# A fused cross-attention and FP4 feed-forward kernel: last rows in two half blocks, first block by feature chunks, small work on GpSimd, softmax ahead of quantisation

## The chip, the core and the metric

The kernel runs on one core of one Trainium2 chip. The metric is the device time of one execution in microseconds (us); runs are compared by their medians. TensorE is called PE here, VectorE DVE, ScalarE ACT, GpSimd POOL and SyncE SP.

## What is computed

The input x has 2 x 2048 rows of 512, and each of the two batches has 77 text tokens. Every row is layer-normalised, projected, and compared with each token of its batch by an additive attention score: a tanh of a 512-vector, dotted with w. The softmax over the tokens gives two numbers, a gate and a shift, for the row. Then a gated feed-forward layer (512 to 1408 to 512) runs on values quantised to FP4 in blocks of 16.

```python
txt_proj = einsum('btd,de->bte', ctx, Ws);  feat_proj = einsum('bfd,de->bfe', layernorm(x), W)
h = tanh(txt_proj[:, None] + feat_proj[:, :, None] + b)      # rows x 77 tokens x 512
rho = einsum('bftd,d->bft', h, w) - 1e30 * (1 - mask)
txt_h = softmax(rho) @ ctx
x = x + tanh(txt_h . Wcw + bcw) * layernorm(x) + tanh(txt_h . Wcb + bcb)
# fp4(v): per block of 16: scale = max|v| / 6; v / scale to the nearest of 0, .5, 1, 1.5, 2, 3, 4, 6; times scale
n = fp4(layernorm(x));  g = n @ fp4(w_gate).T;  y = n @ fp4(w_up).T
x = x + fp4(silu(g) * y) @ fp4(w_down).T
```

## The kernel before

**Scores.** The rows are cut into blocks (`BLOCKS`, line 26: four of 1024). The features of a row lie transposed in `featT`, in 4 chunks of 128 partitions; the token's part is a bias per partition. A quad is four tanh instructions of ACT (`tanh_quad`, line 425; 128 x the block's rows each) and the matmuls that dot them with w (`score_quad`, line 537). A quad of 1024 rows has 8 matmul instructions, one of 512 rows would have 4; each is two passes in the trace. A block needs 77 quads (`QPB`) whatever its rows. The tanh results pass through a ring of four places of 512 rows (`hring`): two quads of 1024 rows, or four of 512.

**The feed-forward tiles.** There are 32 tiles of 128 rows. A tile has four gate/up slots (p = 0 to 3, `gate_up`, line 602, 24 matmuls each) and three down slots (p = 4 to 6, `down`, line 615, 33 matmuls in all) for the tile before. DVE prepares the rows (`rows_tile`), multiplies SiLU(gate) by up (`hidden`), quantises (`quantise`, line 679; `quantise_hidden`) and adds the result. SP moves the quantised rows through transposing DMAs (`turn_x`, `turn_h`).

**The order of work** is written out by hand. Each engine runs its own list and waits on semaphores. `slots` (lines 77 to 92) spreads the quads of block k over the slots of the tiles before it: those of block k end at slot 2 of tile `BASE[k] - 2`, and those of the next begin at slot 5 of the same tile. ACT issues up to two quads beyond what PE scores in a slot, before that slot's SiLU (line 472). In tile `BASE[k] - 2` the scores of the block are drained from PSUM (`softmax_drain`), transposed on PE (`softmax_transposes`), shifted by their maximum (`softmax_shift`), and in the next tile summed (`softmax_sums`) and turned into per-row factors (`softmax_factors`), which `rows_tile` of the next block needs.

**The first block** has no tiles beside it. PE turns its rows, projects the text and the four chunks of both halves (`project_head`, order in `FEAT`, line 250), and then scores. Beside the first block's quads lie the preparation of the weights and of the other 24 tiles' features, taken in 12 pairs of tiles (`rows_pair`, `turn_pair`, `copy_pair`, `project_pair`, `features_pair`), one pair every 4.5 quads (line 584), and on DVE the quantisation of 22 weight pieces of 512 columns and 4 of 1408 (lines 831 to 842). Only when all of them are turned (`wd_turned`, line 842) does DVE drain the first block's scores. GpSimd only builds two small constant tables at the start.

`quantise` forms the block scale, its reciprocal and, in lines 699 to 701, the split of the scale into two float16 parts:

```python
step(stt(d, s, SPLIT, s, ALU.mult, ALU.subtract))
step(stt(hi_b, s, SPLIT, d, ALU.mult, ALU.subtract))
step(tt(lo_b, s, hi_b, ALU.subtract))
```

Lines 716 and 717 need the parts, seven instructions further on.

## Time and profile before

| | us |
|---|---|
| median of 3 runs (lowest, highest) | 1726.71 (1726.48, 1731.03) |
| the profiled execution | 1726.88 |
| its span, first to last instruction | 1725.1 |
| ACT busy in the span | 1356.6 (79%) |
| PE busy | 1482.5 (86%) |
| DVE busy | 1103.6 (64%) |
| POOL busy | 2.7 |

Rows of the trace give a start time in us from the span's start, a busy time in us, the engine, the line of the kernel, what is written and read, and how many instructions are merged (x). A bracket behind a row is the idle time in front of it and the instruction that ended it. Stages are told as stretches of the span: to 62 the head, to 415 the first block, to 1445 the three other blocks beside tiles 0 to 22, and after it the tiles that have no tanh beside them.

### The profile page before, as it was taken

What the parts mean: (1) busy time and instruction counts of PE and PEld (TensorE: products, weight loads), DVE (VectorE), ACT (ScalarE), POOL (GpSimd) and SP (SyncE); (2) the same over time, 40 slices, a digit from 0 to 9 for tenths busy, and PEclk for the clock granted to TensorE, in tenths of its full rate; (3) what the DMA queues carried; (4) which work ended last, traced back from release to release, by engine and by line L of the source; (5) the groups of instructions that cost most, each with busy time, mean ns of one, the idle gap of its engine ahead of it and who ended that gap; (6) DMA issues with size and microseconds to landing.
All of it is one profiled execution on the core that took longest, in us unless ns stands there. A gap on an engine that the chain in (4) does not pass through costs nothing.

```text
span 1725.1 us, 23814 instructions
## 1 busy us (share of the span) xinstructions
PE 1482.5 (86%) x9752; PEld 650.2 (38%) x9752; DVE 1103.6 (64%) x1983; ACT 1356.6 (79%) x1398; POOL 2.7 (0%) x18
## 2 busy tenths in 40 slices
PE   5788888766889989888999999899999998688895
PEld 4234444311333333343333333433333334355552
DVE  4679999864474445356655555657555556799994
ACT  1798888899999999969999999799999995100000
POOL 0000000000000000000000000000000000000000
PEclk9999899888999999999999999999999999799997
DMA  4122232331011111210221111102211111132312
GB/s 130 37 61 71 73 70 68 83 63 30 13 24 36 36 24 36 36 36 13 59 34 39 36 36 36 31 9 45 36 36 36 36 36 36 36 71 61 69 42 52
DMA packets 180753, 77.87 MB, mean 45 GB/s; under 512 B 163851, under 2 KB 163851, under 8 KB 180645
## 3 DMA queue, kind: packets, MB, share of 16 engines
q1 hardware_dynamic: 177392, 74.99, 19.4%
q10 hardware_dynamic: 3253, 1.37, 0.3%
q8 instruction: 76, 1.25, 0.3%
q14 instruction: 32, 0.26, 0.0%
HBM read 27.85 MB, written 8.39 MB: 21 GB/s over the span
## 4 chain that ended last, share of the span: by engine, by line
ACT 59%; DVE 27%; PE 11%; issue 1%; ACTq 1%; DMA 1%; DVEq 0%; SPq 0%
ACT hring L438 56%; DVE work L703 4%; PE rho L548 3%; DVE work L714 2%; DVE work L715 2%; DVE sm L694 2%; ACT sg L458 2%; DVE work L908 1%; DVE work L712 1%; DVE work L713 1%; DVE sm L697 1%; PE dn L623 1%; DVE work L717 1%; DVE work L716 1%; DVE bn L754 1%
## 5 line engine op out<-in xcount | busy, mean ns | idle before, releaser
L438 ACT ACTIVATE hring<-featT,bias 128x1024 f32<-128x1024 f32 x1232 | 1293.0, 1141 | 78.2 <-PE rho L548 73.5
L548 PE MATMUL rho<-hring,wslide 128*32 128x512 f32 x4928 | 618.9, 626 | 135.1 <-ACT hring L438 135.1
L548 PEld LDWEIGHTS rho<-hring,wslide 128*32 128x32 f32 x4928 | 133.5, 112 | 503.3 <-ACT hring L438 274.4
L623 PE MATMUL dn<-wd_room,turned 128*128 128x512 f16 x1056 | 243.9, 383 | 12.8 <-DMA turned<-work 12.8
L908 DVE TENSOR_TENSOR work<-sg,gu1u 128x352 f32<-128x352 f32 x64 | 33.4, 521 | 298.5 <-ACT sg L458 298.0
L623 PEld LDWEIGHTS dn<-wd_room,turned 128*128 128x128 f16 x1056 | 99.2, 99 | 174.7 <-issue 54.8
L611 PE MATMUL gu0g<-wg,turned 128*128 128x352 f16 x768 | 129.6, 320 | 35.7 <-DVE work L908 19.7
L458 ACT ACTIVATE sg<-gu0g 128x352 f32<-128x352 f32 x64 | 29.0, 453 | 153.3 <-PE gu0u L611 153.2
L611 PE MATMUL gu1g<-wg,turned 128*128 128x352 f16 x768 | 128.3, 318 | 0.0
L611 PE MATMUL gu0u<-wu,turned 128*128 128x352 f16 x768 | 126.2, 315 | 0.0
L611 PE MATMUL gu1u<-wu,turned 128*128 128x352 f16 x768 | 125.0, 313 | 0.0
L908 DVE TENSOR_TENSOR work<-sg,gu0u 128x352 f32<-128x352 f32 x64 | 33.4, 521 | 139.7 <-ACT sg L458 138.6
L611 PEld LDWEIGHTS gu0g<-wg,turned 128*128 128x128 f16 x768 | 72.0, 99 | 114.8 <-issue 37.5
L611 PEld LDWEIGHTS gu1g<-wg,turned 128*128 128x128 f16 x768 | 72.5, 99 | 77.4 <-issue 40.9
L703 DVE TENSOR_TENSOR work<-work,sm 128x1408 f32<-128x1408 f32 x34 | 93.9, 2762 | 1.2
L611 PEld LDWEIGHTS gu0u<-wu,turned 128*128 128x128 f16 x768 | 75.8, 99 | 40.5
L611 PEld LDWEIGHTS gu1u<-wu,turned 128*128 128x128 f16 x768 | 75.1, 98 | 39.4
L458 ACT ACTIVATE sg<-gu1g 128x352 f32<-128x352 f32 x64 | 29.1, 454 | 68.0 <-PE gu1u L611 68.0
L714 DVE TENSOR_TENSOR work<-work 128x1408 f32<-128x1408 f32 (+1 forms) x56 | 70.5, 1259 | 1.9
L715 DVE TENSOR_TENSOR work<-work 128x1408 f16<-128x1408 f32 (+1 forms) x56 | 70.5, 1258 | 1.9
L694 DVE TENSOR_REDUCE sm<-work 128x88 f32<-128x1408 f32 x34 | 55.1, 1620 | 1.2
L697 DVE RECIPROCAL sm<-sm 128x88 f32<-128x88 f32 (+1 forms) x90 | 44.4, 493 | 3.1
(147 smaller groups left out, 1019.6 us busy)
## 6 DMA issues: line engine op xcount, KB each, us to landing
xt<-in_x SPq DMA_DIRECT2D x32, 256.0 KB, 2.9
out<-xt SPq DMA_DIRECT2D x32, 256.0 KB, 2.3
work<-in_x SPq DMA_DIRECT2D x10, 512.0 KB, 4.6
xt<-in_x SPq DMA_DIRECT2D x6, 512.0 KB, 3.8
xt<-in_L_ffn_w_gate SPq DMA_DIRECT2D x11, 256.0 KB, 2.6
xt<-in_L_ffn_w_up SPq DMA_DIRECT2D x11, 256.0 KB, 3.5
work<-in_L_ffn_w_down SPq DMA_DIRECT2D x2, 704.0 KB, 4.3
xt<-in_L_ffn_w_down SPq DMA_DIRECT2D x2, 704.0 KB, 4.9
```

What stands on the lines that cost most here:

```text
L438: act.activation(hring[:, s // 2, g, (s % 2) * 512:(s % 2) * 512 + rows], featT[:, e, ROW0[k]:ROW0[k] + rows], ACT.Tanh, bias=bias[:, e, b ...
L458: act.activation(sg[:, n % 2, :], gu[n % 2][0][:, 0:GU_N], ACT.Silu, scale=1.0 / W_PRE).then_inc(sg_ready, 1)
L548: last = pe.matmul(rho[SLOTW * g:SLOTW * g + SLOTW, hf * 512:hf * 512 + 512], wslide[:, e, SLOTW - 1 - r:2 * SLOTW - 1 - r], hring[:, s // ...
L611: last = pe.matmul(ps[:, 0:GU_N], xqT[:, a, k, :], w[:, bb, k, n * GU_N:n * GU_N + GU_N], start=(k == 0 and i == 0), stop=(k == KC - 1 and ...
L623: last = pe.matmul(dn[:, :], hqT[:, a, c, :], wd[:, bb, c, :], start=(c == 0 and i == 0), stop=(c == NC - 1 and i == 2))
L694: step(dve.tensor_reduce(am, v, axis=AX_X, op=ALU.max, apply_absolute_value=True))
L697: step(dve.reciprocal(r, s))
L703: ins = tt(a.rearrange("p (i q b) -> p i b q", **natural), src.rearrange("p (i b q) -> p i b q", **natural), r.rearrange("p (i b) -> p i b ...
L712: step(ts(m.bitcast(I32), a.bitcast(I32), 0x7F800000, None, ALU.bitwise_and))
L714: step(tt(a, a, m, ALU.add))
L715: step(tt(q, a, m, ALU.subtract))
L908: signal(tt(h, sg[:, n % 2, :], gu[n % 2][1][:, 0:GU_N], ALU.mult), gu_drained[n % 2], 2 * t + n // 2 + 1)
```

## The change

`BLOCKS` becomes (1024, 1024, 1024, 512, 512): the last 1024 rows are two blocks, of tiles 24 to 27 and 28 to 31. A quad of the two small blocks has tanh instructions of 128 x 512. The first block's quads run chunk by chunk (`quad_at`), and of the projections only chunk 0 and half of chunk 1 stand ahead of the first score; the others, the text projections of chunks 1 to 3 and the one for the gates stand between quads. A pair of tiles comes every 5 quads from quad 8 on. GpSimd splits the scales of all 90 quantisations and normalises the rows of the pairs, with DVE computing only their statistics. Small loads are issued by SP instead of ACT. In the tile where a block's quads end, drain, transposes and shift stand ahead of `quantise_hidden`, and the next block's quads begin at slot 3.

```diff
-BLOCKS = (1024, 1024, 1024, 1024)
+BLOCKS = (1024, 1024, 1024, 512, 512)
 PRE_QUADS = 7
...
-        if q < 2 * KC:
-            return q % 2, q // 2
+        if q < KC * KC:
+            return q % KC, q // KC
         return q // KC, q % KC
...
-        t0, p0 = (0, 0) if k == 1 else (BASE[k - 1] - 2, 5)
+        t0, p0 = (0, 0) if k == 1 else (BASE[k - 1] - 2, 3)
...
+        feat_bank = [[gu[1][0][:, :], gu[1][1][:, :]], [tr[:, :], dn[:, :]]]
+        text_bank = [gu[0][e % 2][:, 0:BATCH * TOK] for e in range(KC)]
+        uv_bank = gu[0][0][:, 0:2 * BATCH * TOK]
...
+            for n, src in enumerate((w_in, b_in, Wcw_in, Wcb_in)):
+                flat = src.rearrange("a b -> (a b)")
+                sp.dma_start(cols[:, n, :], flat.rearrange("(k p) -> p k", p=P),
+                             allow_slow_non_contiguous=True).then_inc(loaded_c, 16)
+            for n, src in enumerate((bcw_in, bcb_in)):
+                sp.dma_start(bc[:, n:n + 1], src.rearrange("(a n) -> a n", a=1).broadcast_to([P, 1])).then_inc(loaded_c, 16)
...
+            def split(n):
+
+                nb = n // QB
+                s, t, d = sm[:, 1, 0:nb], split_t[:, 0:nb], split_d[:, 0:nb]
+                splits[0] += 1
+                pool.wait_ge(scale_ready, splits[0])
+                small(pool.tensor_scalar(t, s, SPLIT, 1.0, ALU.mult, ALU.mult))
+                small(pool.tensor_tensor(d, t, s, ALU.subtract))
+                small(pool.tensor_tensor(s_hi[:, 0:nb], t, d, ALU.subtract))
+                pool.tensor_tensor(s_lo[:, 0:nb], s, s_hi[:, 0:nb], ALU.subtract).then_inc(split_ready, 1)
+                pool.wait_ge(split_ready, splits[0])
+
+            def normalise_pair(p):
+
+                pool.wait_ge(pair_stats, p + 1)
+                t0 = HEAD_T + 2 * p
+                for j in range(2):
+                    pool.tensor_scalar(xpair[p % 2][:, j, :], xpair[p % 2][:, j, :], nmean[:, j:j + 1],
+                                       rstd[:, t0 + j:t0 + j + 1], ALU.add, ALU.mult).then_inc(pair_normal, 1)
+                pool.wait_ge(pair_normal, 2 * p + 2)
+
+            normalise_pair(0)
+            split(D)
+            split(D)
+            for w in range(1, NC):
+                split(D)
+                normalise_pair(w)
+                split(D)
+            normalise_pair(NC)
+            for r in range(KC):
+                split(INNER)
+            split(D)
+            for t in range(NT):
+                if t + 1 < NT:
+                    split(D)
+                split(INNER)
+
...
-            for e in range(KC):
-                act.wait_ge(text_filled, e // 2 + 1)
-                act.activation(bias[:, e, :], gu[0][e // 2][:, (e % 2) * BATCH * TOK:(e % 2 + 1) * BATCH * TOK],
-                               ACT.Identity, bias=cols[:, 1, e:e + 1]).then_inc(bias_ready, 1)
+            act.wait_ge(text_filled, 1)
+            act.activation(bias[:, 0, :], text_bank[0], ACT.Identity, bias=cols[:, 1, 0:1]).then_inc(bias0_ready, 1)
             copy_head(1)
-            act.wait_ge(bias_ready, KC)
+            act.wait_ge(bias0_ready, 1)
...
-                if k == 0 and q < 2 * KC and q % 2 == 0:
-                    act.wait_ge(feat_ready, feat_at(q // 2))
+                if k == 0 and q < KC * KC and q % KC == 0:
+                    act.wait_ge(feat_ready, 2 * (q // KC) + 2)
+                    if q > 0:
+                        act.wait_ge(bias_ready, q // KC)
...
+                    if t - 1 in SOFTMAX_AT and n == 0:
+                        softmax_exp(SOFTMAX_AT[t - 1])
                     silu_gate(t, n)
-                    if t - 1 in SOFTMAX_AT and n == 1:
-                        softmax_exp(SOFTMAX_AT[t - 1])
...
+            project_text(0)
             pe.wait_ge(loaded_w, 16)
-            pe.wait_ge(bias_ready, KC)
-            project_head(0)
-            project_head(1)
+            project_head(0, 0)
             turn_head(1)
-            for i in range(2, len(FEAT)):
-                project_head(i)
...
+            project_head(0, 1)
+            project_text(1)
+            project_head(1, 0)
...
-                pe.wait_ge(xn_ready, HEAD_T + 2 * p + 2)
+                pe.wait_ge(pair_normal, 2 * p + 2)
                 if p == 0:
-                    pe.wait_ge(uv_ready, 1)
...
+                if n == 0:
+                    project_head(1, 1)
+                if n == 2:
+                    project_text(2)
+                    project_head(2, 0)
+                if n == 3:
+                    project_head(2, 1)
+                if n == 5:
+                    project_text(3)
+                    project_head(3, 0)
+                if n == 6:
+                    project_head(3, 1)
+                if n == 7:
+                    project_uv()
                 for w in range(PAIRS + 1):
-                    at = 5 + (9 * w) // 2
+                    at = 8 + 5 * w
...
-                    if t in SOFTMAX_AT and p == 5:
+                    if t in SOFTMAX_AT and p == 3:
                         softmax_transposes(SOFTMAX_AT[t], 0)
-                    if t - 1 in SOFTMAX_AT and p == 0 and halves(SOFTMAX_AT[t - 1]) == 2:
-                        softmax_transposes(SOFTMAX_AT[t - 1], 1)
                     for n in slots.get((t, p), ()):
                         score_quad(n)
+                    if t in SOFTMAX_AT and p == 3 and halves(SOFTMAX_AT[t]) == 2:
+                        softmax_transposes(SOFTMAX_AT[t], 1)
...
+                scales[0] += 1
+                signal(ts(s, am, pre / FP4_MAX, least * pre, ALU.mult, ALU.max), scale_ready, scales[0])
                 step(dve.reciprocal(r, s))
                 step(ts(r, r, pre * TIE_DOWN, None, ALU.mult))
-                step(stt(d, s, SPLIT, s, ALU.mult, ALU.subtract))
-                step(stt(hi_b, s, SPLIT, d, ALU.mult, ALU.subtract))
-                step(tt(lo_b, s, hi_b, ALU.subtract))
 
...
+                dve.wait_ge(split_ready, scales[0])
...
-            rows_pair(0)
-            for w in range(NC + KC):
-                if w < NC:
-                    gate_up_weights(w)
-                else:
-                    down_weights(w - NC)
-                if w < PAIRS:
-                    copy_pair(w)
-                if 0 < w <= PAIRS:
-                    features_pair(w - 1)
-                if w + 1 < PAIRS:
-                    rows_pair(w + 1)
...
+            gate_up_weights(0, 0)
+            text_bias(2)
+            features_head(2)
+            gate_up_weights(0, 1)
+            text_bias(3)
+            features_head(3)
+            text_gates()
+            for w in range(NC - 1):
+                copy_pair(w)
+                gate_up_weights(w + 1, 0)
+                stats_pair(w + 1)
+                if w > 0:
+                    features_pair(w - 1)
+                gate_up_weights(w + 1, 1)
+            copy_pair(NC - 1)
+            stats_pair(NC)
+            features_pair(NC - 2)
+            down_weights(0)
+            copy_pair(NC)
+            features_pair(NC - 1)
+            down_weights(1)
+            down_weights(2)
+            features_pair(NC)
+            down_weights(3)
...
                 hidden(t, 0)
-                if ending is not None and halves(ending) == 2:
-                    softmax_shift(ending, 1)
                 hidden(t, 1)
                 if ending is not None:
                     softmax_sums(ending)
                 elif t + 1 < NT:
                     rows_tile(t + 1)
                 hidden(t, 2)
+                if begun is not None:
+                    softmax_drain(begun)
+                    softmax_shift(begun, 0)
                 hidden(t, 3)
+                if begun is not None and halves(begun) == 2:
+                    softmax_shift(begun, 1)
                 if ending is not None:
                     softmax_factors(ending)
                     rows_tile(t + 1)
-                if begun is not None:
-                    softmax_drain(begun)
                 quantise_hidden(t)
                 if t > 0:
                     result(t - 1)
                 if begun is not None:
-                    softmax_shift(begun, 0)
                     restart()
             result(NT - 1)
 
```

**On PE, at the start of the program** (gu, tr and dn are PSUM banks; stage and wd_room hold the turned rows of the two halves, turned holds W). Before:

```order
L517 MATMUL gu0g<-wd_room 128x154 x8
L517 MATMUL gu0u<-wd_room 128x154 x8
L507 MATMUL gu0g<-stage,turned 128x512 x4
L507 MATMUL gu1g<-stage,turned 128x512 x4
L507 MATMUL gu0u<-wd_room,turned 128x512 x4
L507 MATMUL gu1u<-wd_room,turned 128x512 x4
L507 MATMUL gu0g<-stage,turned 128x512 x4
L507 MATMUL gu0u<-wd_room,turned 128x512 x4
L507 MATMUL gu1g<-stage,turned 128x512 x4
L507 MATMUL gu1u<-wd_room,turned 128x512 x4
L532 MATMUL tr<-wd_room,xt 128x154 x8
L548 MATMUL rho<-hring,wslide 32x512 x48
```

In the change:

```order
L573 MATMUL gu0g<-wd_room 128x154 x4
L563 MATMUL gu1g<-stage,turned 128x512 x4
L563 MATMUL gu1u<-wd_room,turned 128x512 x4
L573 MATMUL gu0u<-wd_room 128x154 x4
L563 MATMUL tr<-stage,turned 128x512 x4
L609 MATMUL rho<-hring,wslide 32x512 x8
L563 MATMUL dn<-wd_room,turned 128x512 x4
L609 MATMUL rho<-hring,wslide 32x512 x16
L573 MATMUL gu0g<-wd_room 128x154 x4
L563 MATMUL gu1g<-stage,turned 128x512 x4
```

Ahead of the first score stand three half chunks of 128x512 in place of eight, and two text projections of 128x154 x4 in place of four; five half chunks and two text projections went between the first quads.

**On DVE, around the drain of a block's scores in tile 6.** Before:

```order
L908 TENSOR_TENSOR work<-sg,gu1u 128x352
L847 TENSOR_SCALAR stage<-rho,negm 128x1024
L694 TENSOR_REDUCE sm<-work 128x88
...
L716 TENSOR_TENSOR work<-work,s_hi 128x1408
L717 TENSOR_TENSOR work<-work,s_lo 128x1408
L920 SCALAR_TENSOR_TENSOR xt<-dn,xt 128x512
L854 TENSOR_REDUCE mx<-tr 128x4
L855 TENSOR_TENSOR stage<-tr,mx 128x512
L908 TENSOR_TENSOR work<-sg,gu0u 128x352
L854 TENSOR_REDUCE mx<-tr 128x4
L855 TENSOR_TENSOR stage<-tr,mx 128x512
```

In the change:

```order
L1013 TENSOR_TENSOR work<-sg,gu0u 128x352
L952 TENSOR_SCALAR stage<-rho,negm 128x1024
L959 TENSOR_REDUCE mx<-tr 128x4
L960 TENSOR_TENSOR stage<-tr,mx 128x512
L1013 TENSOR_TENSOR work<-sg,gu1u 128x352
L959 TENSOR_REDUCE mx<-tr 128x4
L960 TENSOR_TENSOR stage<-tr,mx 128x512
L769 TENSOR_REDUCE sm<-work 128x88
...
L791 TENSOR_TENSOR work<-work,s_lo 128x1408
L1025 SCALAR_TENSOR_TENSOR xt<-dn,xt 128x512
```

Both shifts moved ahead of the 14 (now 11) instructions of the quantisation and of the result, and the drain moved ahead of the second half's last `hidden` product.

**On ACT, in tiles 14 to 22 and 22 to 26 of the change** (sg is the SiLU of a gate/up slot). In the first stretch:

```order
L516 ACTIVATE sg<-gu0g 128x352
L496 ACTIVATE hring<-featT,bias 128x512 x4
L516 ACTIVATE sg<-gu1g 128x352
L496 ACTIVATE hring<-featT,bias 128x512 x8
L516 ACTIVATE sg<-gu0g 128x352
L496 ACTIVATE hring<-featT,bias 128x512 x8
L516 ACTIVATE sg<-gu1g 128x352
L496 ACTIVATE hring<-featT,bias 128x512 x16
```

In the second:

```order
L496 ACTIVATE hring<-featT,bias 128x512 x12
L516 ACTIVATE sg<-gu0g 128x352
L496 ACTIVATE hring<-featT,bias 128x512 x12
L516 ACTIVATE sg<-gu1g 128x352
L496 ACTIVATE hring<-featT,bias 128x512 x40
L516 ACTIVATE sg<-gu0g 128x352
L496 ACTIVATE hring<-featT,bias 128x512 x12
L516 ACTIVATE sg<-gu1g 128x352
```

The tanh instructions between two SiLUs are half as wide as before in both; in the second stretch there are about twice as many of them in a tile.

## Rows read from the trace of the kernel before

**Rows 1.** The page's part 4, the chain that ended last: shares by engine.

```profile
ACT 59%; DVE 27%; PE 11%; issue 1%; ACTq 1%; DMA 1%; DVEq 0%; SPq 0%
```

**Rows 2.** Busy time by stretch: stretch, length, PE, PEld, DVE, ACT, POOL, clock, DMA, GB/s.

```profile
62.20:414.90 352.70, 274.65 (x1728) 123.31 (x1720) 282.84 (x636) 322.70 (x309) 0.00 (x0) 0.89 0.28 68
...
1101.50:1445.50 344.00, 318.87 (x2239) 127.92 (x2238) 199.73 (x321) 327.62 (x337) 0.00 (x0) 0.99 0.16 35
1443.50:1501.40 57.90, 38.10 (x218) 21.62 (x218) 42.38 (x85) 6.80 (x13) 0.00 (x0) 0.86 0.15 33
1501.40:1725.10 223.70, 188.00 (x1065) 105.91 (x1065) 188.42 (x275) 14.83 (x32) 0.00 (x0) 0.94 0.26 57
```

**Rows 3.** Waits from 62.2 to 414.9: who waited for whom, total us, times, longest.

```profile
ACT hring L438 <- PE rho L548: 41.9, 24, 11.9
...
PE tr L563 <- DVE xt L736: 19.4, 5, 4.3
DVE stage L847 <- PE rho L548: 18.7, 1, 18.7
```

**Rows 4.** Waits from 414.9 to 1443.5.

```profile
ACT hring L438 <- PE rho L548: 31.6, 8, 9.4
```

**Rows 5.** Timelines of DVE, ACT and PE in the head.

```profile
20.77 2.29 DVE L736 TENSOR_SCALAR work<-work,stat,rstd 128x512 f32<-128x512 f32 x4
...
41.90 8.42 ACT L438 ACTIVATE hring<-featT,bias 128x1024 f32<-128x1024 f32 x8 [4.65 <-DVE featT L749]
...
51.15 3.60 PE L507 MATMUL gu1g<-stage,turned 128*128 128x512 f32 x8
...
62.20 50.01 ACT L438 ACTIVATE hring<-featT,bias 128x1024 f32<-128x1024 f32 x48 [11.88 <-PE rho L548]
```

**Rows 6.** Groups of instructions: shapes, count, busy us, mean ns, idle before.

```profile
L438 ACT ACTIVATE hring<-featT,bias 128x1024 f32<-128x1024 f32 x1232 | 1293.0, 1141 | 78.2 <-PE rho L548 73.5 <-DVE featT L749 4.6
...
L458 ACT ACTIVATE sg<-gu1g 128x352 f32<-128x352 f32 x64 | 29.1, 454 | 68.0 <-PE gu1u L611 68.0
...
L699 DVE SCALAR_TENSOR_TENSOR sm<-sm 128x88 f32<-128x88 f32 (+1 forms) x90 | 19.4, 216 | 3.1
...
L446 ACT ACTIVATE stage<-stage 128x512 f32<-128x512 f32 x8 | 4.7, 623 | 0.3 <-DVE stage L855 0.3
```

**Rows 7.** Groups of POOL.

```profile
L363 POOL TENSOR_SCALAR_AFFINE_SELECT gat<-gat 128x1 f32<-128x1 f32 (+1 forms) x7 | 1.4, 200 | 1.0
...
L369 POOL TENSOR_SCALAR_AFFINE_SELECT idf<-idf 128x128 f32<-128x128 f32 x1 | 0.3, 293 | 0.2 <-POOL idf L367 0.2
```

**Rows 8.** The chain of waits beside the first block, by start and us.

```profile
111.41 0.70 DVE featT L773
...
118.29 0.70 DVE sm L694
...
124.92 0.70 DVE sm L694
```

**Rows 9.** Timeline of DVE at the first block's end.

```profile
408.70 1.28 DVE L847 TENSOR_SCALAR stage<-rho,negm 128x1024 f32<-128x1024 f32 x1 [18.74 <-PE rho L548]
```

**Rows 10.** The chain of waits, PE's pieces beside the second block.

```profile
614.82 2.05 PE dn L623 x9
616.87 1.85 PE rho L548 x16
618.72 1.90 PE gu0g L611 x12
620.62 1.79 PE gu0u L611 x12
```

**Rows 11.** The chain of waits in the tiles without tanh.

```profile
1526.15 2.72 DVE work L703
...
1550.39 2.72 DVE work L703
```

**Rows 12.** Waits from 1440 to 1520.

```profile
PE tr L599 <- DVE stage L855: 6.7, 1, 6.7
```

More of the change, by code:

```diff
@@ L51, in bass_xattn_fp4_ffn @@
     assert sum(BLOCKS) == BATCH * SEQ and D == 512 and NC == 11 and TOK == GRP * FULLR + 1 and HEAD_T == 8
-    assert BATCH_OF == [(r + n - 1) // SEQ for r, n in zip(ROW0, BLOCKS)]
+    assert PAIRS == NC + 1 and BATCH_OF == [(r + n - 1) // SEQ for r, n in zip(ROW0, BLOCKS)]
     def halves(k):
@@ L248, in bass_xattn_fp4_ffn @@
         down_free = sem("down_free")
-        FEAT = [(0, 0), (1, 0), (0, 1), (1, 1), (2, 0), (2, 1), (3, 0), (3, 1)]
-        def feat_at(e):
-            return max(i for i, (ee, _) in enumerate(FEAT) if ee == e) + 1
+        FEAT = [(e, hh) for e in range(KC) for hh in range(2)]
         block = ctx.enter_context(nc.Block())
@@ L295, in _ @@
             for i in range(NC):
+                if 2 <= i < PAIRS:
+                    sp.wait_ge(pair_turned, i - 1)
+                    passed()
+                    load_pair(i)
                 for m in range(2):
@@ L381, in _, with small @@
                 unit(gat[:, FULLR:FULLR + 1], -(SLOTW * g + FULLR), [[0, 1]], 2 * g + 1)
+            steps, splits = [0], [0]
+            def small(ins):
+                steps[0] += 1
+                ins.then_inc(split_step, 1)
+                pool.wait_ge(split_step, steps[0])
+            def split(n):
[30 more added lines that the diff above has]
+                split(INNER)
         @block.scalar
@@ L498, in turn_head, with project_head, project_text, project_uv @@
                     last.then_inc(head_turned, 1)
-            def project_head(i):
-                e, hh = FEAT[i]
+            def project_head(e, hh):
                 pe.wait_ge(xnT_ready, 4 * hh + 4)
-                again = [j for j in range(i) if FEAT[j][0] % 2 == e % 2 and FEAT[j][1] == hh]
-                if again:
-                    pe.wait_ge(feat_ready, again[-1] + 1)
+                if e >= 2:
+                    pe.wait_ge(feat_ready, 2 * (e - 2) + hh + 1)
                 for k in range(KC):
-                    last = pe.matmul(gu[e % 2][hh][:, :], Wf[:, k, e * P:e * P + P], xnT4[hh][:, k, :],
+                    last = pe.matmul(feat_bank[e % 2][hh], Wf[:, k, e * P:e * P + P], xnT4[hh][:, k, :],
                                      start=(k == 0), stop=(k == KC - 1))
                 last.then_inc(feat_filled, 1)
+            def project_text(e):
+                if e == 2:
+                    pe.wait_ge(bias0_ready, 1)
+                if e == 3:
+                    pe.wait_ge(bias_ready, 1)
+                for k in range(KC):
+                    last = pe.matmul(text_bank[e], Wsf[:, k, e * P:e * P + P], ctxT[:, k, :],
+                                     start=(k == 0), stop=(k == KC - 1))
+                last.then_inc(text_filled, 1)
+            def project_uv():
+                pe.wait_ge(wcol_ready, 1)
+                pe.wait_ge(bias_ready, 2)
+                for u in range(2):
+                    for k in range(KC):
+                        last = pe.matmul(uv_bank[:, u * BATCH * TOK:(u + 1) * BATCH * TOK], wcol[:, u, k, :],
+                                         ctxT[:, k, :], start=(k == 0), stop=(k == KC - 1))
+                last.then_inc(uv_filled, 1)
             turn_head(0)
@@ L655, in _ @@
         def _(dve):
-            done = [0]
+            done, scales = [0], [0]
             def step(ins):
@@ L681, in quantise @@
                 nb = n // QB
-                am, s, r, d = (sm[:, i, 0:nb] for i in range(4))
+                am, s, r = (sm[:, i, 0:nb] for i in range(3))
                 hi_b, lo_b = s_hi[:, 0:nb], s_lo[:, 0:nb]
@@ L724, in rsqrt @@
                 step(ts(y.bitcast(I32), t.bitcast(I32), -1.0, float(RSQRT_SEED), ALU.mult, ALU.add))
-                for _ in range(3):
+                for i in range(3):
                     step(tt(t, y, y, ALU.mult))
                     step(stt(t, t, -0.5, a, ALU.mult, ALU.mult))
-                    step(stt(y, t, 1.5, y, ALU.add, ALU.mult))
+                    ins = stt(y, t, 1.5, y, ALU.add, ALU.mult)
+                    if i == 2 and last:
+                        return ins
+                    step(ins)
             def normalise(t0, src, n):
@@ L754, in rows_pair @@
                     step(dve.bn_stats(bn[:, j, :], xpair[p % 2][:, j, :]))
-                normalise(HEAD_T + 2 * p, [xpair[p % 2][:, j, :] for j in range(2)], 2)
+                for j in range(2):
+                    step(dve.bn_aggr(stat[:, t0 + j, :], bn[:, j, :]))
+                if p > 0:
+                    dve.wait_ge(pair_normal, 2 * p)
+                step(ts(nmean[:], stat[:, t0:t0 + 2, 0:1].rearrange("p t a -> p (t a)"), -1.0, None, ALU.mult))
+                signal(rsqrt(rstd[:, t0:t0 + 2], stat[:, t0:t0 + 2, 1:2].rearrange("p t a -> p (t a)"), 2, last=True),
+                       pair_stats, p + 1)
             def copy_pair(p):
```

119 lines of the change are left out of this document (58 added, 61 removed).

## The prediction

> **What bounds the kernel now.** I read the chain of waits first: ACT has 59% of it, DVE 27%, PE 11% [rows 1]. Then the busy times by stretch [rows 2] say where each of them decides. Beside the three later blocks (1101.5 to 1445.5 is the last of them) ACT is busy 328 of 344 us: it makes tanh as fast as it can. After the last tanh, at 1443.5, there are 58 us in which nobody is near full, and then 224 us in which ACT has 15 us of work. There DVE decides: the same instruction of DVE returns after 24.25 us, tile after tile [rows 11]. So the tanh that ACT must do, 1232 instructions that follow each other every 1.04 us (50.01 us for 48, [rows 5]), is 1281 us, and the 282 us behind it are tiles that could not start earlier, because their rows' scores came last. The first block, 62 to 415, is a third case: ACT waits there 41.9 us in all for PE to free the ring, PE waits 19.4 us for DVE's normalised rows [rows 3], and DVE is busy 283 of 353 us [rows 2].
>
> The sum is made against the profiled execution, 1726.9 us, which is its span of 1725.1 and 1.8 around it; the median of the three runs is 1726.7. A difference under 0.3%, 5 us, counts as no change.
>
> **The head and the first block.** The first tanh runs at 41.9, two quads fit the ring, and ACT then stands 11.9 us until PE has done all eight half chunks and scores at last [rows 5]. Counted from its restart at 62.2, ACT is as far as if it had started without a pause at 62.2 - 8.3 = 53.9. In the change chunk 0 needs one text projection and two half chunks. DVE's second set of normalised rows is ready at 23.1, unchanged [rows 5]; then PE's turns (1), ACT's copies (1), one half chunk (3.6, [rows 5]) and DVE's copy (0.7) give a first tanh at about 29. The other projections stand between quads. With a score of 1.85 and a half chunk of 3.6 against the 4.16 us of a quad PE falls behind a little; I take 3 us of ACT waiting for the first eight quads, and 0.7 us for each of 12 pairs, 8 us, since a pair is projected in two halves, each as many passes as a half chunk, 3.6 us. ACT alone would thus have done 79 quads at 29 + 79 x 4.16 + 11 = 369.
>
> DVE sets a later end. It drains the first block only when the last weights are turned. Before, that was no matter: DVE had waited 18.7 us for PE [rows 3] when the drain came at 408.7 [rows 9]. A pair costs DVE 1.4 us of copies (two of the 0.70 at 111.41) and 6.9 us of features, statistics and normalisation (111.41 to 118.29), a weight piece 6.6 us (118.29 to 124.92) [rows 8]: 21.6 us for a pair and two pieces, more than the 18.7 us of 4.5 quads. That is where PE's 19.4 us come from. The change takes off 3 x 0.22 us per piece [rows 6] and 1.0 per pair: 19.3 us, against 20.8 for 5 quads. So the pace is ACT's again, but it is a slower pace for the pairs: pair 11 is turned after quad 63, at about 311. Behind it DVE has three of the four large weights (24.25 of a tile, less 7.8 for the next rows, 2.9 for `hidden` and the result, and 0.9 for the split, is 12.7 us; a turn of some 5 us behind each) and the last copies, some 66 us, so it drains at 377. Its first exponentials follow 6.2 us later, as they did (408.7 to 414.9). **The first block ends at 383 in place of 415: -32 us**, and not the 46 of ACT's own account. GpSimd's pieces are costed at nothing here: a split is needed 4.3 us after its scale, and the nearest rows of POOL are 0.20 us for one column and 0.29 for 128 [rows 7], so four small instructions are about 1 us.
>
> **Blocks 2 and 3.** In these 1030.6 us (414.9 to the last score at 1445.5) ACT waits 31.6 us, nearly all at two places [rows 4]: where a block's quads end, PE stands in its list before the second transposes until DVE, busy with the 13 us quantisation, has done the first shift. Drain and shifts now stand ahead of it, so the wait goes. I leave 2 us, for the rows of the next block, which still come behind the factors: **-29.6**. Late next is that `hidden` of slot 3 now waits behind the drain, 2 us, which no one misses, as it waited 8 us for ACT's SiLU.
>
> **The last 1024 rows.** Before, they were one block of 8 tiles, bound by ACT: 77 x 4.16 + 32 SiLUs of 0.35 + 4.5 for exponentials and table loads = 336 us. Now the first 512 rows lie beside tiles 14 to 22. A tanh of 512 columns: the nearest row is the exponential, 623 ns against 1141 for 1024 columns [rows 6], 0.518 us per 512 columns with next to nothing fixed, so 0.52; the upper bound is 0.62, what one takes alone. ACT needs 77 x 2.08 + 11 + 5 = 176 us. PE needs per tile four slots of 1.90 + 1.79 = 3.7, 7.5 for the down products (2.05 for 9 of 33) and 9.6 scores of 0.93: 31.2 us [rows 10]; 8 tiles, with transposes and one turn, are 252 us. DVE's 24 lie below. So PE bounds, at 252. Then tiles 22 to 26 take the second 512 rows: ACT 160 + 16 x 0.35 + 4 = 170, PE 4 x 31.2 + 36 = 161; they are near each other, ACT may be only 4.2 us ahead where it was 8.3, so I add 0.5 us per gate/up slot: 177. **429 in place of 336: +93.** This is the price of the smaller blocks, and the return is below.
>
> **Behind the last tanh.** From the last score to the first tile of the last block it is 55.9 us before. PE's 6.7 us for the shift [rows 12], the second half's sums (six instructions of 0.7, 4.1) and the splits (1.5) go: **-12.3**. Then come 223.7 us for eight tiles [rows 2]; four remain, 4 x 24.25 less: **-97.0**. The splits would save 1.5 us of DVE per tile, 6 us; POOL's part is not known, between 0 and 6, and I take **-3**.
>
> The sum: 1726.9 - 32 - 29.6 + 93 - 12.3 - 97 - 3 = 1646.
>
> **GpSimd beside DVE.** Rows 7 show POOL only where DVE is idle; whether the two hinder each other stands in no row. If each of POOL's instructions held DVE for its own length, a split would cost 4 x 0.25 = 1.0 against 0.65 to 0.85 saved, and a normalisation of a pair (0.57 us for 512 columns, on from rows 7) 1.15. The Trainium skill, "SBUF — State Buffer", section on SBUF's two separate sides, states that GpSimd shares a port pair with VectorE's two-input and two-port instructions, as an exclusive lock for a whole instruction. By that rule the trace's silence is no comfort: most of `quantise` behind the scale is of such instructions, and the time would be that of the first rival.
>
> **The rivals.**
> 1. *POOL holds DVE up.* 22 x 1.0 + 4 x 1.1 + 12 x 1.15 = 40 us more of DVE in the first block; the slack of 1.5 us at each of 10 pairs absorbs 14: +26. In the tail the 3 us are not had and 4 to 5 tiles pay 1.6 more: +10. 1682. For it: 180 groups of small instructions between dependent ones of DVE. Against it: they are short.
> 2. *The first block keeps its end,* because pairs come later and the large weights follow in a row: an early start is then worth nothing. 1678. For it: DVE's 283 of 353 us. Against it: the 19.4 us that PE waited.
> 3. *Two quads ahead are too little* with tanh of 2.08 us a quad: ACT and PE take turns in waiting, 36 us in place of 31.2 in eight tiles, 47 in place of 44 in four: +54, 1700. Against it: in the first stretch ACT has 76 us to spare.
> 4. *Better than the sum:* DVE's end does not bind (-8), ACT and PE do not hinder each other in tiles 22 to 26 (-8), the splits are gained whole (-3): about 1625.
> 5. *Slower than before: the split outlasts its cover.* DVE then stands before the first of the two last products of every quantisation. 26 lie in the first block, some 10 in tiles where DVE decides. To lose the 81 us, and the slack of 14, each must stand 2.6 us, so four small POOL instructions must take 6.9 us, 1.7 each. It costs nothing up to 1.07 us each. Against it: 0.2 to 0.3 [rows 7].
>
> **How the numbers follow.** The sum 0.50, better 0.12, POOL in the way 0.14, first block unmoved 0.09, turns in waiting 0.10, slower 0.05. The likeliest is the sum, 1646. From 1618 to 1694 holds it, the better case, rivals 1 and 2 and the near half of 3. The exponential's upper bound for a 512-wide tanh (0.62) lies within it: +31 in tiles 22 to 26. Faster by over 0.3%: 0.94; within: 0.01; slower: 0.05.
>
> **What would show it.** Tanh from about 29 without a gap of 10 us. The drain of the first block at 375 to 380, DVE not waiting ahead of it. Waits of ACT for PE of 1 to 3 us at the block ends. Tiles 14 to 22 at 31 us with PE over 95% busy and ACT under 75%; tiles 22 to 26 at 44 with ACT over 93%. The last tiles at 23 to 24 us. Wrong would be DVE instructions of two inputs that take longer than before, a pause ahead of the scaled products, or the eight tiles at over 34 us.

## The result and the profile after

The changed kernel takes **1680.0 us**, the median of 4 runs (1678.51 to 1684.74), against 1726.6 of the kernel before in the same comparison (1726.26 to 1731.03): a ratio of 0.973 with an interval of 0.970 to 0.975. It is faster, as forecast, and inside the range, but 34 us above the 1646 of the sum. The profiled execution took 1678.5 us, 32.5 above the sum. Its page, the busy times and the chain's shares:

```profile
PE 1464.5 (87%) x9752; PEld 634.0 (38%) x9752; DVE 1045.3 (62%) x1725; ACT 1417.2 (85%) x1707; POOL 254.2 (15%) x402
...
ACT 52%; PE 33%; DVE 13%; DMA 2%; issue 1%; SPq 0%; DVEq 0%; ACTq 0%
```

Against [rows 1] the chain runs half as much over DVE (13% for 27%) and three times as much over PE (33% for 11%). The stretches, in the columns of [rows 2]:

```profile
388.40:1051.50 663.10, 603.04 (x4294) 238.57 (x4295) 347.81 (x510) 660.82 (x680) 81.75 (x120) 0.99 0.16 32
1051.50:1308.00 256.50, 250.19 (x1641) 111.22 (x1641) 186.23 (x266) 203.97 (x341) 42.78 (x63) 1.00 0.23 48
1308.00:1512.00 204.00, 171.70 (x1167) 64.35 (x1164) 101.62 (x155) 200.58 (x333) 23.49 (x34) 0.99 0.14 30
...
1552.80:1676.40 123.60, 97.06 (x549) 54.18 (x549) 96.82 (x120) 7.41 (x16) 23.53 (x32) 0.93 0.26 57
```

Blocks 2 and 3 are bound by ACT (661 of 663 us), tiles 14 to 22 by PE (250 of 256.5, ACT 80%), tiles 22 to 26 by ACT again (200.6 of 204), and the last 124 us by DVE's chain.

**The first block.** The timelines of ACT, DVE and PE (start, us, instruction, idle before it and what ended that), where [rows 5] and [rows 9] stood before:

```profile
30.00 20.90 ACT L496 ACTIVATE hring<-featT,bias 128x1024 f32<-128x1024 f32 x20 [4.65 <-DVE featT L826]
...
384.28 0.63 ACT L504 ACTIVATE stage<-stage 128x512 f32<-128x512 f32 x1 [11.71 <-DVE stage L960]
387.89 0.63 ACT L504 ACTIVATE stage<-stage 128x512 f32<-128x512 f32 x1 [2.98 <-DVE stage L960]
...
380.67 2.05 PE L674 MATMUL tr<-gat,stage 128*128 128x128 f32 x8 [14.44 <-DVE stage L952]
...
379.24 1.28 DVE L952 TENSOR_SCALAR stage<-rho,negm 128x1024 f32<-128x1024 f32 x1 [0.15 <-DVE marker L746]
```

The first tanh is at 30.0 (the prediction said 29), the drain at 379.2 (377) with no wait of DVE for PE ahead of it, and the first exponential at 384.3 (383). PE stood 14.4 us for that drain and ACT 11.7, so DVE does end this block. ACT waits a second time, 3.0 us, for the other half. Tanh is back at 388.4, where it was at 416.3 before, 28 us for 32 forecast. ACT's tanh before and then in the change:

```profile
416.31 8.40 ACT L438 ACTIVATE hring<-featT,bias 128x1024 f32<-128x1024 f32 x8
388.43 8.41 ACT L496 ACTIVATE hring<-featT,bias 128x1024 f32<-128x1024 f32 x8
```

**The blocks' ends.** The waits from 388.4 to 1443, beside the 31.6 of [rows 4]:

```profile
ACT hring L496 <- PE rho L609: 1.1, 2, 0.8
```

Of the 31.6 us before, only 16.4 lie up to the end of block 3. The second long wait, at its end, falls behind its last score, in the stretch of the last block; PE and ACT of the kernel before:

```profile
1093.80 1.96 PE L611 MATMUL gu1g<-wg,turned 128*128 128x352 f16 x12
...
1105.97 8.42 ACT L438 ACTIVATE hring<-featT,bias 128x1024 f32<-128x1024 f32 x8 [5.08 <-PE rho L548]
...
1123.94 4.27 ACT L438 ACTIVATE hring<-featT,bias 128x1024 f32<-128x1024 f32 x4 [9.20 <-PE rho L548]
```

Block 3's last score ends at 1093.8 there (the first row is what PE does next). From the return of tanh to that score it is 677.5 us before and 663.0 in the change: 14.5 less. The last 1024 rows took 351.7 us before, with the other 15.2 of the waits in them.

**The last 1024 rows.** The chain in order of time (start, us, engine and line, number of instructions):

```profile
1260.81 2.05 PE dn L698 x9
...
1292.54 2.05 PE dn L698 x9
...
1315.54 22.05 ACT hring L496 x36
...
1416.83 24.49 ACT hring L496 x40
...
1557.97 2.87 DVE work L776
...
1580.84 2.89 DVE work L776
```

A tile of the PE-bound stretch takes 31.7 us (31.2 forecast). In tiles 22 to 26, 36 tanh of 512 columns take 22.05 us, and 40 take 24.49: one every **0.612 us**, not every 0.52. Behind the last tanh DVE's cadence is 22.87 us a tile, against 24.25 in [rows 11]. The groups, in the columns of [rows 6]:

```profile
L496 ACT ACTIVATE hring<-featT,bias 128x1024 f32<-128x1024 f32 x924 | 969.9, 1154 | 18.4 <-PE rho L609 13.4 <-DVE featT L826 4.7
L496 ACT ACTIVATE hring<-featT,bias 128x512 f32<-128x512 f32 x616 | 382.1, 710 | 0.0
```

Half the width is 710 ns for 1154, 62% and not half.

The time by stretches (profiled executions; each begins where the one above ends). The first forecast is the 1445.5 of the last score less the prediction's 336 for the last block, less 32 and 29.6:

| Stretch | forecast, us | measured, us | off |
|---|---|---|---|
| to block 3's last score (1051.4) | 1047.9 | 1051.4 | +3.5 |
| tiles 14 to 22, to 1311.3 | 252 | 259.8 | +8 |
| tiles 22 to 26, to 1512.1 | 177 | 200.8 | +24 |
| to tile 28's first products, 1558.2 | 43.6 | 46.1 | +2.5 |
| to the end | 123.7 | 118.2 | -5.5 |

The 24 us are most of the miss; the others add up to 8.

### The profile page after: what moved, and what is told of

Read it like the earlier page. It is cut to its first block, busy times and chain, and to the rows that moved or that the text cites. A ratio compares the mean times of both kernels' runs of the same rounds, so it can differ in the third digit from the quotient of the medians.

```text
span 1676.4 us, 24460 instructions
## 1 busy us (share of the span) xinstructions
PE 1464.5 (87%) x9752; PEld 634.0 (38%) x9752; DVE 1045.3 (62%) x1725; ACT 1417.2 (85%) x1707; POOL 254.2 (15%) x402
## 3 DMA queue, kind: packets, MB, share of 16 engines
q10 hardware_dynamic: 693, 1.36, 0.3%
## 4 chain that ended last, share of the span: by engine, by line
ACT 52%; PE 33%; DVE 13%; DMA 2%; issue 1%; SPq 0%; DVEq 0%; ACTq 0%
ACT hring L496 49%; PE rho L609 11%; PE dn L698 5%; PE gu1g L686 3%; PE gu1u L686 2%; PE gu0g L686 2%; DVE work L776 2%; PE gu0u L686 2%; ACT sg L516 1%; PE gu0u L636 1%; PE gu0g L636 1%; DVE work L787 1%; DVE work L788 1%; DVE sm L769 1%; PE gu1g L636 1%; PE gu1u L636 1%
## 5 line engine op out<-in xcount | busy, mean ns | idle before, releaser
L496 ACT ACTIVATE hring<-featT,bias 128x1024 f32<-128x1024 f32 (+1 forms) x1540 | 1352.0, 976 | 18.4 <-PE rho L609 13.4
L609 PEld LDWEIGHTS rho<-hring,wslide 128*32 128x32 f32 x4928 | 127.6, 110 | 500.8 <-ACT hring L496 310.4
L423 POOL TENSOR_SCALAR split_t<-sm 128x88 f32<-128x88 f32 (+1 forms) x90 | 22.0, 245 | 1260.1 <-DVE sm L772 1260.0
L426 POOL TENSOR_TENSOR s_lo<-sm,s_hi 128x88 f16<-128x88 f32 (+1 forms) x90 | 121.4, 1349 | 7.1
L776 DVE TENSOR_TENSOR work<-work,sm 128x1408 f32<-128x1408 f32 x34 | 99.8, 2935 | 1.2
```

Source lines behind the costliest of these rows:

```text
L423: small(pool.tensor_scalar(t, s, SPLIT, 1.0, ALU.mult, ALU.mult))
L426: pool.tensor_tensor(s_lo[:, 0:nb], s, s_hi[:, 0:nb], ALU.subtract).then_inc(split_ready, 1)
L496: act.activation(hring[:, s // 2, g, (s % 2) * 512:(s % 2) * 512 + rows], featT[:, e, ROW0[k]:ROW0[k] + rows], ACT.Tanh, bias=bias[:, e, b ...
L609: last = pe.matmul(rho[SLOTW * g:SLOTW * g + SLOTW, hf * 512:hf * 512 + 512], wslide[:, e, SLOTW - 1 - r:2 * SLOTW - 1 - r], hring[:, s // ...
L776: ins = tt(a.rearrange("p (i q b) -> p i b q", **natural), src.rearrange("p (i b q) -> p i b q", **natural), r.rearrange("p (i b) -> p i b ...
```

## The experiments

Twelve kernels, in three groups. Ratios are against the kernel before on the same chip, with their intervals; its median was 1727.6 to 1728.9 us in the three groups.

**The change without its half blocks**, from the changed kernel:

```diff
-BLOCKS = (1024, 1024, 1024, 512, 512)
+BLOCKS = (1024, 1024, 1024, 1024)
```

> The change with its blocks alone undone (four of 1024). My theory after the result: the half blocks cost more than they give, because a tanh of 512 columns follows the next after 0.61 us and not 0.52. From the last score of block 3 to the last score of all it is 460.6 us in the change's trace; a single block of 1024 needs 337. Four tiles more without tanh are 4 x 22.9 = 92, and a second half's sums 4. So 1680 - 124 + 92 + 4 = 1652, faster than the change. Rival (the prediction's own terms, +93 against -97 and -4): the blocks give 8 us, so it would be 1688.

It took 1652.1 us (1651.0 to 1652.9), ratio 0.956 (0.955 to 0.957). So the half blocks cost the change 28 us; the sum had them at a gain of 8.

**The half blocks alone**, the reverse edit of `BLOCKS` in the kernel before:

> The kernel before with its blocks alone changed (1024 x 3, 512 x 2). My theory: 461 us and a second place where PE waits for the shift, in place of 352, against 4 x 24.25 + 4 saved: 1727 + 109 + 8 - 101 = 1743, slower than before by about 1%. Rival (the prediction's terms): 1727 + 93 - 101 = 1719, or the same within 8 us.

1745.6 us, ratio 1.010 (1.009 to 1.012): a loss of 17 us here. It is less than 28 because the shorter tail is worth more in the kernel before. Behind the last drain it saves 107.6 us here (167.1 for 274.7) and 93.8 in the change (164.1 for the 257.9 of four blocks), where each of the four tiles takes 22.88 us and not 24.25 (5.5 of the 14 us; the rest was not traced). The last 1024 rows, from the third block's drain to the last, cost about as much in both: 127.6 us more here (476.4 for 348.8) and 122.1 in the change (460.7 for 338.6).

**The splits back on DVE** (GpSimd keeps the rows of the pairs):

```diff
-                scales[0] += 1
-                signal(ts(s, am, pre / FP4_MAX, least * pre, ALU.mult, ALU.max), scale_ready, scales[0])
+                step(ts(s, am, pre / FP4_MAX, least * pre, ALU.mult, ALU.max))
...
+                step(stt(d, s, SPLIT, s, ALU.mult, ALU.subtract))
+                step(stt(hi_b, s, SPLIT, d, ALU.mult, ALU.subtract))
+                step(tt(lo_b, s, hi_b, ALU.subtract))
...
-                dve.wait_ge(split_ready, scales[0])
...
```

> The change with the splits of the scales back on DVE (three instructions each; GpSimd only normalises the pairs' rows). If the splits on GpSimd are gained nearly whole: 1.4 us per tile in about five tiles where DVE decides, and some 6 us in the first block, 1680 + 13 = 1693, with 24.3 us from tile to tile at the end. Rival, POOL takes the port from DVE as often as it helps: 1680 within 3 us, with 22.9 from tile to tile unchanged.

1695.3 us, ratio 0.981 (0.980 to 0.983): the splits on GpSimd are worth 15 us. Rival 1 of the prediction, by which they cost time, falls with it.

**The softmax in its old places** on PE, ACT and DVE (drain behind the factors, first shift behind `quantise_hidden`, second transposes in the next tile, exponentials behind slot 1's SiLU):

```diff
-        t0, p0 = (0, 0) if k == 1 else (BASE[k - 1] - 2, 3)
+        t0, p0 = (0, 0) if k == 1 else (BASE[k - 1] - 2, 5)
...
-                if begun is not None:
-                    softmax_drain(begun)
-                    softmax_shift(begun, 0)
                 hidden(t, 3)
```

> The change with the order around the softmax undone (next block's quads from slot 5, drain and shifts behind the quantisation, exponentials one SiLU later). Theory: two waits of ACT for PE of 15 us come back, at the ends of blocks 2 and 3, about 7 us where a half block follows a half block and 8 to 12 behind the last tanh: 1680 + 45 = 1725. Rival: in the stage where PE decides and behind the last tanh it changes nothing, so +30, 1710.

1706.1 us, ratio 0.987 (0.986 to 0.989): the order is worth 26 us, less than either of the expected 45 and 30. From one block's drain to the next it is 341.5, 347.7, 269.1 and 208.3 us here, and 334.0, 338.4, 261.2 and 199.5 in the change: 7.5 to 9.3 us for each block. They add up to more than 26, as a drain of the old order also stands further behind its last score. Taken at the last score it is 29 us (1541.1 for 1512.1), and what follows is 1.9 us shorter in the old order. Part of the gain is ACT's waits for PE from 388 to 1500, in this kernel:

```profile
ACT hring L496 <- PE rho L609: 16.0, 4, 8.8
```

**What makes the narrow tanh dear.** First the text's column, taken from the half blocks' tanh, so that this kernel leaves the token's part out of the last 1024 rows:

```diff
-                                   bias=bias[:, e, base + tok:base + tok + 1]).then_inc(tanh_ready, 1)
+                                   bias=(bias[:, e, base + tok:base + tok + 1] if rows > 512 else 0.0)).then_inc(tanh_ready, 1)
```

> The change, with the tanh of the two half blocks given a constant 0.0 as bias in place of the token's column: it leaves out the token's part for the last 1024 rows. If the 0.18 us that a 512-wide tanh has beyond half a 1024-wide one come from reading a new bias column, the spacing falls from 0.61 to about 0.53, and tiles 22 to 26 from 201 to 177 us: 1656. Rival, they are a fixed part of every such instruction: 0.61 and 1680 stay.

One run, 1660.6 us. Its chain, in the same stretch:

```profile
1317.65 18.70 ACT hring L496 x36
```

That is 0.519 us apiece, the 0.52 of the forecast. Tiles 22 to 26 of this kernel, in the columns of [rows 2]:

```profile
1313.40:1495.40 182.00, 163.85 (x1145) 64.21 (x1142) 98.57 (x151) 169.67 (x327) 22.22 (x32) 1.00 0.17 34
```

They take 182 us, for 200.8 with the column and 177 forecast. ACT is busy 93% and PE 90% there, and neither alone fills the stretch. Then the signals, one for a quad in place of four:

```diff
...
-                                   bias=bias[:, e, base + tok:base + tok + 1]).then_inc(tanh_ready, 1)
+                                          bias=bias[:, e, base + tok:base + tok + 1])
+                last.then_inc(tanh_ready, 1)
...
-                pe.wait_ge(tanh_ready, GRP * (n + 1))
+                pe.wait_ge(tanh_ready, n + 1)
```

> The change, with one semaphore signal per quad in place of one per tanh. If the fixed part comes from signalling, the spacing of the 512-wide tanh falls to about 0.53 (1656), and that of the 1024-wide to under 1.0. Rival: 0.61 and 1.04 stay, and the time is 1680 within 3 us, since PE waits for whole quads anyway.

1681.9 us, ratio 0.973 (0.971 to 0.975), within the spread of the change; the group's mean stayed at 709 ns. Signals cost nothing that shows here.

**Does the column cost every tanh, and does it cost because it changes?** Once no tanh has a column (`bias=0.0`), once all narrow ones read the same (`bias[:, 0, 0:1]`):

> The change with bias 0.0 in every tanh of the scores: it leaves out the token's part everywhere. Without a bias column a 512-wide tanh followed after 0.519 us, with one after 0.612. If a column costs 0.09 us in any width, the 1024-wide falls from 1.04 to 0.95, the stages that ACT bounds lose up to 0.09 x 600 = 55 us, and it comes to about 1605 to 1620. Rival: 0.519 is half of 1.04, so the column's cost is hidden behind a long instruction, 1.04 stays, and the time is that without bias in the half blocks alone, 1660.

> The change, with the tanh of the half blocks all given the same bias column from SBUF (wrong tokens' part for the last 1024 rows). If what costs is that the column changes from one instruction to the next: 0.52 and 1660. If any column from SBUF costs: 0.61 and 1680.

Without any column: one run, 1617.1 us, and in the chain of that kernel

```profile
504.21 22.72 ACT hring L496 x24
```

24 tanh of 1024 columns at 0.947 us, against the 1.042 of [rows 5] (50.01 for 48). With the same column throughout: one run, 1683.6 us, and in its chain

```profile
1372.67 22.05 ACT hring L496 x36
```

0.612 us, as in the change. So a column costs 0.093 to 0.095 us an instruction at both widths, and at 512 columns it is the same whether it changes or not.

**Does DVE end the first block?** Four blocks, splits on GpSimd, and the pairs closer together; then closer still:

```diff
-                    at = 8 + 5 * w
+                    at = 8 + (14 * w) // 3
```

> Four blocks of 1024 as in the first experiment, and a pair of tiles every 4.67 quads in place of 5. Theory: the first block's end is DVE's, and DVE's large weights start when the last pair is through, which now comes 4 quads earlier; with 19.3 to 19.9 us of DVE against 19.4 of 4.67 quads it follows nearly. The drain of the first block comes at about 369 in place of 379: 10 us faster than four blocks with pairs every 5 quads. Rival: DVE is full, PE then waits for it as before the change, and the drain stays where it is.

1637.6 us (1636.4 to 1637.9), ratio 0.947 (0.945 to 0.949), 14.5 less than with pairs every 5 quads. Its timeline of DVE, and below it the waits of its first block, from 62 to 390:

```profile
363.09 0.06 DVE L746 MEMSET marker<- 128x1 f32 x1 [5.36 <-DMA wd_room<-work]
368.86 1.28 DVE L952 TENSOR_SCALAR stage<-rho,negm 128x1024 f32<-128x1024 f32 x1 [5.71 <-PE rho L609]
```

```profile
ACT stage L504 <- DVE stage L960: 2.0, 1, 2.0
...
PE tr L674 <- DVE stage L952: 1.5, 1, 1.5
```

The weights are done at 363 (379 in the change), DVE now waits 5.7 us for PE, and the waits of ACT and PE for DVE, 15.1 and 12.8 us with pairs every 5 quads, have shrunk to 2.0 and 1.5. DVE's own waits for the pairs' turned rows fell from 20.9 us to 8.0, which shows that it was the pairs' distance that held it up.

```diff
-                    at = 8 + 5 * w
+                    at = 8 + (9 * w) // 2
```

> Four blocks and a pair every 4.5 quads, as before the change. DVE needs 19.3 to 19.9 us for a pair and two weight pieces, 4.5 quads are 18.7: DVE would be full and PE wait for it, so no better than 4.67 quads within 3 us (1637), with PE waiting for POOL's or DVE's rows again. Rival: PE's 2 quads less move the end by another 8 us, 1630.

1636.5 us, ratio 0.947 (0.946 to 0.949). DVE's wait ahead of the drain grows to 9.6 us and the drain comes at 365.0, but the whole differs by 1.1 us, under the 0.3% that the prediction takes as no change: DVE is no longer the end.

**The parts apart.** Four blocks with the splits on DVE, and then this with the softmax in its old places too, which leaves of the change only the first block's order, GpSimd's rows and the loads (the edits are those above):

> Four blocks of 1024 and the splits on DVE. There are eight to ten tiles in which DVE decides: if a split on GpSimd gives 1.4 us per tile there, this is 4 x 1.4 = 6 us worse against four blocks than the half blocks were in the same exchange, about +19 against four blocks. Rival: no more than with the half blocks.

> Four blocks, splits on DVE, softmax in the old order: what is left of the change is the first block's new order with pairs every 5 quads and their rows normalised by GpSimd. If the parts add up: 1728 - 33 + 2 = about 1697 (1652 + 15.7 for the splits + 30 for the softmax order). Rival, the parts work against each other: over 3 us from that.

1667.8 us, ratio 0.965 (0.963 to 0.966), and 1701.6 us, ratio 0.985 (0.983 to 0.986). The splits are worth 15.7 us here, near the 15.3 with half blocks and not the 19 expected. Why shows in the chain behind the last tanh, with the splits on GpSimd (four blocks) and then on DVE:

```profile
1462.22 2.89 DVE work L776
...
1485.10 2.89 DVE work L776
```

```profile
1471.68 0.91 DVE work L776
...
1495.92 0.91 DVE work L776
```

(L776 of the second kernel is another instruction of the same quantisation.) A tile takes 22.88 us against 24.24, 1.36 us less. With two gaps of 24.9 among the seven of the tail, these are 160.2 us against 171.0. The earlier drain of the first block (379.7 for 381.8) is 2.1 more. The rest, about 3 us, lies outside these gaps in the same stretch, which is 257.9 us from the last drain to the end, for 272.0. The ladder is then:

| Kernel | median, us | step |
|---|---|---|
| before | 1728.6 | |
| + first block's order, GpSimd's rows | 1701.6 | -27 |
| + softmax ahead of quantisation | 1667.8 | -34 |
| + splits on GpSimd | 1652.1 | -16 |
| + half blocks (the change) | 1680.0 | +28 |
| instead of them: pairs every 4.67 quads | 1637.6 | -14.5 |

The first step holds the order of the quads, the pairs' rows on GpSimd and the small loads on SP together; they were not tried apart. In its own comparison it is 26 us (1727.6 before). It came 4.6 us off its expectation: the softmax order gives 34 us with four full blocks and 26 with half blocks, so the parts are not quite additive. From drain to drain it is 343.3, 351.6 and 348.7 us with the old order and 335.7, 338.3 and 338.3 with the new: 7.6, 13.3 and 10.4 us for a block of 1024 rows. But this pair of kernels has its splits on DVE and the other pair on GpSimd, and already the end of block 3, where the row blocks are alike, gains 13.3 here and 9.3 there. Whether the blocks or the splits make the 8 us of difference was not tried. The best kernels of the study are the two with denser pairs, 5.3% faster than before and 42 us faster than the change.

## Why the prediction was right, and where it was not

**Right: first block.** The forecast was -32 by the drain of DVE and not the -46 of ACT's account. The drain came 2 us late, ACT's second wait of 3.0 us for the other half was not in the sum (it was 0.3 before), and 28 were gained. That the weights on DVE set this end is shown: with closer pairs the drain moved by 11 us and the kernel by 14.5. Rival 2, the first block unmoved, is refuted. What I took as given, the pairs' distance, was an opportunity of its own: the prediction itself had 19.3 us of DVE's work against 20.8 for 5 quads, and a third of a quad, 1.4 us, at each of eleven pairs makes 15 of the 16 us by which the weights came earlier.

**Right: the blocks' ends.** The waits went from 31.6 to 1.1 us, with 2 forecast. Undoing the order costs 26 us over the whole kernel. The prediction booked them wrongly, though: blocks 2 and 3 gained 14.5 us and not 29.6, and the last 1024 rows were 351.7 us and not 336, because the second wait lay in the last block. In the sum the two slips, 15 and 16 us, cancel.

**Wrong: "a tanh of 512 columns ... so 0.52".** This is the term that failed, in the last 1024 rows: +93 was +125 on the prediction's base (259.8 + 200.8 - 336). Tiles 22 to 26 have 308 narrow tanh, and 308 x 0.092 is 28 us of ACT's time. Of these 19 were on the path: without the column the stretch is 182 us for 200.8, and the kernel 19.4 us faster. The other 5 us of the 24 stay without the column, in a stretch in which ACT and PE each wait for the other; for that the sum had 7 us (170 to 177), and it takes 12. The row that I took as nearest, the exponential of [rows 6], adds no column, and the difference 1141 - 623 is the cost of 512 columns *and* of one bias column, which I read as columns alone. The SiLU of the same rows, 454 ns for 352 columns, has none either. The upper end, 0.62, was near the right one; the +31 that the prediction gave for it was too much for what the column did, 19 us, since PE too is 90% busy in the stretch without it. The Trainium skill has the price, in "ScalarE: Activation LUTs", section "What ACT_TABLE_LOAD costs": an ACTIVATE takes 186 ns and 0.833 ns a column, each pointer operand adds about 93 ns, and neighbours overlap by about 93. Worked out from that page's figures, an estimate is 613 ns between narrow tanh with a column and 520 without, and the runs show 612 and 519. I had not weighed that rule.

**Half right: tiles 14 to 22.** PE bounds them at 31.7 us a tile, near the 31.2, with ACT busy 80% and not under 75. Most of the 8 us beyond 252 are an idle PE in the first two tiles:

```profile
1060.00:1140.00 80.00, 74.37 (x480) 31.54 (x479) 67.55 (x106) 62.26 (x103) 14.63 (x20) 1.00 0.18 39
1140.00:1308.00 168.00, 168.00 (x1109) 74.74 (x1108) 114.53 (x156) 133.67 (x224) 28.14 (x43) 1.00 0.26 52
```

PE stands 5.6 us there and not at all behind. The chain runs over DVE from 1079 to 1117, through the sums, the factors, the next block's first rows and two quantisations; the sum had no term for that. Even at 0.52 the half blocks would have lost: without the column in the narrow tanh the kernel takes 1660.6, and four full blocks with every column 1652.1. My reading, which no run isolates, is that ACT idles a fifth of 256 us while PE bounds, and that the four tiles saved behind do not pay it back.

**Off on the good side: the splits.** -3 was taken "between 0 and 6" for the tail. They are gained nearly whole, 1.36 us of the 1.5 in each of its tiles, and the whole move is worth 15 us. The last stretch was 5.5 us under its forecast.

**The rivals.** *POOL holds DVE up* is refuted as a loss, and in an instructive way. The timeline of DVE and POOL in the last tiles:

```profile
1580.84 2.88 DVE L776 TENSOR_TENSOR work<-work,sm 128x1408 f32<-128x1408 f32 x1
...
1580.33 0.37 POOL L424 TENSOR_TENSOR split_d<-split_t,sm 128x88 f32<-128x88 f32 x1
...
1580.78 0.37 POOL L425 TENSOR_TENSOR s_hi<-split_t,split_d 128x88 f16<-128x88 f32 x1
...
1581.23 2.57 POOL L426 TENSOR_TENSOR s_lo<-sm,s_hi 128x88 f16<-128x88 f32 x1
```

POOL's last instruction, of the same 88 columns as the 0.37 us ones, takes 2.57 and ends at 1583.80, with DVE's product at 1583.72. The two do exclude each other, as "SBUF — State Buffer" of the Trainium skill says, in its section on the two separate sides: the trace agrees. But the loser is POOL, because DVE's long instruction has started; DVE's product is the sign of being wrong that the prediction named, an instruction of two inputs that takes longer than before. It took 2935 ns in the mean, 2762 before, and 2758 in the kernel with the splits back on DVE (the groups in this order):

```profile
L776 DVE TENSOR_TENSOR work<-work,sm 128x1408 f32<-128x1408 f32 x34 | 99.8, 2935 | 1.2
L703 DVE TENSOR_TENSOR work<-work,sm 128x1408 f32<-128x1408 f32 x34 | 93.9, 2762 | 1.2
L766 DVE TENSOR_TENSOR work<-work,sm 128x1408 f32<-128x1408 f32 x34 | 93.8, 2758 | 1.2
```

So the hindrance is there, 0.17 us a quantisation of 1408 columns, and it is small beside the instructions that left DVE. A rule of exclusion has a direction, and I priced it only in the direction that hurts. *The split outlasts its cover* is refuted as well: even with 2.6 us in it, the split is done when `quantise` asks, and no wait of DVE for it shows. *Two quads ahead are too little* did not decide: ACT is 98% busy in its stretch and PE 98% in the other, and only the kernel without the column shows some 5 us of it. Its price of 54 us does not come out of its own figures either: 8 x 36 + 4 x 47 less 252 and 177 is 47. *Better than the sum* was right only in the splits.

## What to carry to other kernels

Before halving a tile, take the fixed part of an instruction from the same form, operands included: a group with a bias column and one without differ by more than their columns. Where one engine's account sets a stage's end, look at how evenly the work that feeds it is laid out, since moving it closer can be worth more than making it smaller. A tail that is shortened by smaller blocks has to be weighed with what the small blocks cost where they are worked on, here 122 us for 94.

## What the runs showed of the hardware

- A bias column costs ACT 0.093 to 0.095 us an instruction, at 512 and at 1024 columns, and at 512 the same column as much as a new one: 1617.1 us for the kernel without any against 1680.0. A signal on every tanh costs nothing that shows.
- A tensor_tensor of GpSimd that starts during DVE's two-input product of 1408 columns ends with it: 0.37 us became 2.57. The normalisation of 512 columns took 768 ns on GpSimd, against the 0.57 that I had from [rows 7].
- PE's eight transposes took 2.05 us after its pause of 14.4 us, at a granted clock of 0.60 from 380.67 to 384.90, a mean that lies nearer to the lower of its two levels (1.2 and 2.4 GHz, or 0.5 and 1.0). With a pause of 1.5 us, in the kernel with closer pairs, they took 1.13 at a clock of 1.00. It is a small further price of DVE's late drain. The windows of the changed kernel, the pause and what follows it:

```profile
366.30:380.60 14.30, 0.00 (x0) 0.00 (x0) 8.50 (x9) 6.27 (x7) 0.43 (x1) 0.64 0.42 94
380.67:384.90 4.23, 4.23 (x24) 2.27 (x24) 1.38 (x2) 0.62 (x1) 0.00 (x0) 0.60 0.27 98
```
